# Two graph convolutions of a four-layer graph network: 90 of 125 superblocks placed and swept by cells, the rows of the other blocks fetched by GpSimd inside the same sweep

## The chip, the cores and the metric

The kernel runs on one core of a Trainium2 chip. A core has five engines that run side by side, each with its own instruction queue: TensorE (PE, the matrix multiplier), VectorE (DVE), ScalarE (ACT), GpSimd (POOL) and SyncE (SP, which only starts transfers); they wait for each other by semaphores. The metric is the time of one execution on the device, in microseconds, as the median of three runs.

## What is computed

A graph of 12,500 nodes with 32 features and 400,000 edges (`src`, `dst`) goes through four layers; each ends with a residual and a layer norm. The change touches the third, two graph convolutions in a row:

```python
def gcn_conv(x, W, b, row, col, n_nodes):
    xw = x @ W
    deg = jax.ops.segment_sum(ones, col, num_segments=n_nodes)
    dinv = jnp.where(deg > 0, jax.lax.rsqrt(deg), 0.0)
    norm = dinv[row] * dinv[col]
    msgs = norm[:, None] * xw[row]
    out = jax.ops.segment_sum(msgs, col, num_segments=n_nodes)
    return out + b
...
h = jax.nn.relu(gcn_conv(x, W1, b1, row, col, n))
h = jax.nn.relu(gcn_conv(h, W2, b2, row, col, n))
```

What costs time is `segment_sum(xw[row], col)`, once for each convolution: for each edge the row of its source is read and added to the row of its target. The norms are applied to whole nodes before and after.

## The kernel before

The edges are cut into 625 blocks of 640 (5 tiles of 128). The targets of a block lie close together, within a window of 64 nodes. Five blocks make a superblock, so there are 125.

The layers on either side (`weighted_edges`, `coupled_edges`) and `conv_edges` go block by block. POOL fetches the source rows with five indirect transfers (128 rows of 128 bytes each), DVE makes a one-hot matrix of the targets (`onehot`, 128x320), PE multiplies rows by one-hot, and DVE adds the resulting window to the sums.

The two convolutions share another way. `place_edges` runs once and sorts the edges of each superblock into cells: source node `100*row + bin` goes to bin `bin`, and each of the 100 bins has 64 places. Its loop over 125 superblocks (`rank_and_spread`, L1024 to L1058) is a chain of DVE instructions, with two POOL instructions (L896, L900) and 52 matmuls beside it. It stores, for each superblock, the source row of each place (`cells`) and the target (`cell_dst`). Edges that found no place stay in `rest`.

`cell_sweep` then runs once for each convolution, over the 125 superblocks, each in two halves of 50 bins. SP loads the source rows of a half, broadcast to all partitions (`src`, L1141, 800 KB). DVE compares them with the lane number (`from_row`, L1213) and makes 25 one-hot tiles of targets (`to_dst`, L1220, 128x224, bf16). PE picks the rows out of a table that stays in SBUF (`gather`, L1163, 50 matmuls a half), ACT copies them to SBUF (L1201), PE multiplies them by `to_dst` (`scatter`, L1176, 25 matmuls a half), and DVE adds the sum to `conv_acc` (L1231). The order is written out by hand: DVE makes half h+1 and then adds half h; PE runs two packs of gathers ahead of its scatters. POOL does nothing here. After each sweep `conv_edges` takes what is left in `rest`, here one turn of four blocks (L1287, L1307, L1321).

The address of each add comes from a table in SBUF that DVE's sequencer loads into registers (`base_of`, L406).

## Time and profile before

| | us |
|---|---|
| median of three runs | 18041.62 (18037.58 to 18050.91) |
| the profiled execution | 18071.57 |
| its span, first to last instruction | 18069.8 |
| stages up to the placing | 8258 |
| `place_edges` | 2129 |
| first sweep, with its preparation | 1572 |
| `conv_edges` and the node stage between | 231 |
| second sweep, with its preparation | 1577 |
| the rest | 4303 |

The profile gives each instruction's engine, start, duration and idle time before it. A name with `<-` reads "output from inputs", and L and a number is the line in the listing above. A pack of matmuls is shown as one row with a count. An f32 matmul is recorded twice (x10 are five matmuls).

### The profile page before, as it was taken

The numbers are of one execution on the slowest core, as the hardware profiler recorded it, in microseconds if no ns is written. First come the engines' busy times: TensorE is split into PE (matmuls) and PEld (weight loads), VectorE is DVE, ScalarE is ACT, GpSimd is POOL, SyncE is SP. The second block draws the span as 40 slices with busy tenths as digits, with TensorE's granted clock in tenths as the row PEclk, the third lists the DMA queues.
The fourth block names the chain that finished last, engine by engine and source line by source line (L and its number), as shares of the span: only waits on it lengthen the run. The fifth ranks groups of instructions, "written<-read, shape, count | busy, mean of one in ns | idle before, by whom it ended". The sixth has DMA issues, their size and how long they took to land. (4 is left out here: it accounts for less than half of the span.)

```text
span 18069.8 us, 315870 instructions
## 1 busy us (share of the span) xinstructions
PE 13832.7 (77%) x90210; PEld 10270.1 (57%) x90210; DVE 14107.8 (78%) x36234; ACT 3512.3 (19%) x6730; POOL 9545.5 (53%) x9706
## 2 busy tenths in 40 slices
PE   7999999997777777774333377777777999999998
PEld 5666666666666666664222255555555555555555
DVE  8999999983333333338999999959998999989996
ACT  1111111111000000001000044434443222222222
POOL 6777777774777777771222200000002777777774
PEclk9888888885555555555555599979998999999998
DMA  1111111110111111110000033313332111111111
GB/s 37 28 28 28 28 28 28 28 27 15 17 17 17 17 17 17 17 17 9 1 1 1 1 129 134 133 62 129 133 133 68 18 18 18 18 18 18 18 18 15
DMA packets 996527, 680.08 MB, mean 38 GB/s; under 512 B 743750, under 2 KB 911411, under 8 KB 995988
## 3 DMA queue, kind: packets, MB, share of 16 engines
q1 hardware_dynamic: 694254, 524.34, 9.9%
q0 software_dynamic: 302240, 155.35, 6.0%
q8 instruction: 15, 0.25, 0.0%
q14 instruction: 18, 0.15, 0.0%
HBM read 669.12 MB, written 9.60 MB: 38 GB/s over the span
## 5 line engine op out<-in xcount | busy, mean ns | idle before, releaser
L529 PE MATMUL weighted_weights_ps<-weighted_w_out,weighted_hidden 128*128 128x256 f32 x12600 | 3891.1, 436 | 591.0 <-DVE weighted_to_s L654 515.0
L529 PEld LDWEIGHTS weighted_weights_ps<-weighted_w_out,weighted_hidden 128*128 128x128 f32 x12600 | 2328.3, 205 | 2444.8 <-issue 1634.8
L740 PE MATMUL coupled_win<-coupled_onehot,coupled_prod 128*125 128x64 f32 x12500 | 2785.3, 419 | 1142.7 <-DVE coupled_prod L788 1142.7
L359 POOL DMA_INDIRECT weighted_rows<-x_after_convolved,weighted_idx x3140 | 3039.3, 968 | 1045.6 <-issue 942.9
L359 POOL DMA_INDIRECT weighted_rows<-in_x,weighted_idx x3140 | 3028.3, 964 | 1013.6 <-issue 935.5
L725 POOL DMA_INDIRECT coupled_rows<-x_after_weighted,coupled_idx x3125 | 2955.5, 946 | 1146.0 <-issue 952.3
L740 PEld LDWEIGHTS coupled_win<-coupled_onehot,coupled_prod 128*125 128x125 f32 x12500 | 2670.8, 329 | 1257.2 <-DVE coupled_prod L788 1257.2
L1220 DVE TENSOR_SCALAR cells_to_dst<-from,cells_current 128x224 bf16<-128x224 bf16 x12500 | 2389.9, 273 | 18.1
L784 DVE TENSOR_TENSOR coupled_prod<-coupled_harm,coupled_rows 128x640 f32<-128x640 f32 x625 | 515.4, 825 | 2381.1 <-DMA coupled_rows<-x_after_weighted,coupled_idx 2381.1
L1176 PE MATMUL cells_sum_ps<-cells_to_dst,cells_rows 128*96 128x224 bf16 x12500 | 1703.6, 267 | 687.6 <-DVE cells_to_dst L1220 687.6
L649 DVE TENSOR_TENSOR weighted_v_v<-weighted_weights_ps,weighted_scaled 128x320 f32<-128x320 f32 x3768 | 1956.2, 573 | 0.0
L1287 POOL DMA_INDIRECT conv_rows<-conv_rows,conv_idx x40 | 38.0, 950 | 3421.4 <-DMA conv_idx<-in_src_blocks 3409.8
L1201 ACT ACTIVATE cells_rows<-cells_rows_ps 128x480 bf16<-128x480 f32 x2500 | 1427.4, 571 | 1733.2 <-PE cells_rows_ps L1163 1733.2
L562 PEld LDWEIGHTS weighted_win_ps<-weighted_onehot,weighted_prod 128*128 128x128 f32 x12560 | 1712.3, 203 | 88.1
L1176 PEld LDWEIGHTS cells_sum_ps<-cells_to_dst,cells_rows 128*96 128x96 bf16 x12500 | 1132.2, 122 | 885.5 <-ACT cells_rows L1201 738.6
L562 PE MATMUL weighted_win_ps<-weighted_onehot,weighted_prod 128*128 128x64 f32 x12560 | 1624.4, 279 | 0.0
L519 PE MATMUL weighted_hid_ps<-weighted_feat,weighted_w_in 32*64 32x320 f32 (+1 forms) x3786 | 1531.4, 485 | 82.7 <-DMA weighted_feat<-in_ef 79.2
L578 ACT ACTIVATE weighted_hidden<-weighted_hid_ps,weighted_b_in 64x320 f32<-64x320 f32 x1262 | 659.4, 523 | 3338.4 <-PE weighted_hid_ps L519 3332.9
L1163 PE MATMUL cells_rows_ps<-cells_parts,cells_from_row 125*64 125x96 bf16 x25000 | 1010.2, 211 | 73.5 <-DVE cells_from_row L1213 73.5
L654 DVE TENSOR_TENSOR weighted_to_s<-weighted_weights_ps,weighted_scaled 128x640 f32<-128x640 f32 x1256 | 1020.4, 812 | 0.0
L661 DVE TENSOR_REDUCE weighted_prod<-weighted_to_s 128x40 f32<-128x640 f32 x1256 | 1016.1, 809 | 0.0
L578 ACT ACTIVATE weighted_hidden<-weighted_hid_ps,weighted_b_mid 64x320 f32<-64x320 f32 x1262 | 659.3, 522 | 1824.8 <-PE weighted_hid_ps L517 1824.8
(204 smaller groups left out, 14514.0 us busy)
## 6 DMA issues: line engine op xcount, KB each, us to landing
cells_src<-cell_sources SPq DMA_DIRECT2D x500, 800.0 KB, 4.1
weighted_feat<-in_ef SPq DMA_DIRECT2D x635, 80.0 KB
weighted_rows<-in_x,weighted_idx POOLq DMA_INDIRECT x3140
weighted_rows<-x_after_convolved,weighted_idx POOLq DMA_INDIRECT x3140
coupled_rows<-x_after_weighted,coupled_idx POOLq DMA_INDIRECT x3125, 2.4
weighted_idx<-in_src_blocks SPq DMA_DIRECT2D x1264, 2.5 KB
weighted_sh<-in_sh SPq DMA_DIRECT2D x1264, 10.0 KB
coupled_sh<-in_sh SPq DMA_DIRECT2D x630, 22.5 KB
```

The lines of the kernel that those rows point to most:

```text
L359: pool.indirect_dma_start(rows[s][:, t, :], None, table, bass.IndirectOffsetOnAxis(ap=idx[s][:, t:t + 1].bitcast(U32), axis=0))\
L519: mm = pe.matmul(hid_ps[0:halves * HID, 0:HALF], w_in[:, :], feat[slot][:, u * HALF:(u + 1) * HALF], start=True, stop=True)
L529: mm = pe.matmul(banks[bank][:, t * WPATHS:(t + 1) * WPATHS], hidden[slot][:, t * P:(t + 1) * P], w_out[:, :], start=True, stop=True)
L562: mm = pe.matmul(win_ps[0:MSG, 0:WINDOW], prod[s][:, t, :], onehot[s][:, t, :], start=(t == 0), stop=(t == TILES - 1))
L578: step = nc.scalar.activation(hidden[slot][0:HID, half * HALF:(half + 1) * HALF], hid_ps[0:HID, 0:HALF], func, bias=(b_mid if deep else b_ ...
L649: last = dve.tensor_tensor(v_v[:, :, m * MUL:(m + 1) * MUL, :], w_vv, v_m[:, :, None, :].broadcast_to([P, TILES, MUL, MUL]), ALU.mult)
L654: dve.tensor_tensor(to_s[:, :, :, :], w_s, scaled[:, :, None, 0:2 * MUL].broadcast_to([P, TILES, MUL, 2 * MUL]), ALU.mult).then_inc(w_used, 1)
L725: pool.indirect_dma_start(rows[s][:, t, :], None, table, bass.IndirectOffsetOnAxis(ap=idx[s][:, t:t + 1].bitcast(U32), axis=0))\
L740: mm = pe.matmul(win_ps[s][0:OCH, c * WINDOW:(c + 1) * WINDOW], prod[s][:, t, c * OCH:(c + 1) * OCH], onehot[s][:, t, :], start=(t == 0), ...
L1176: mm = pe.matmul(sum_ps[h][0:wide, 0:DSTS], rows[b][:, c, :], to_dst[h][:, t, :], start=(t == 0), stop=(t == HALF_TILES - 1))
L1201: nc.scalar.activation(rows[b][:, :, :].rearrange("p c f -> p (c f)"), rows_ps[b][:, 0:PACK * wide], ACT.Copy).then_inc(copied, 1)
L1220: made = dve.tensor_scalar(to_dst[h][:, t, :], k["from1"][:, 0:DSTS], current[h][:, t:t + 1], None, ALU.is_equal)
```

## The change

The placing and both sweeps cover only the first 90 superblocks (450 blocks). The other 178 blocks (175 real ones and 3 that are empty) go by rows, two beside each of the superblocks 0 to 88 of each sweep. For each of them SP loads the source numbers, POOL fetches the rows with five indirect transfers into one of four slots, DVE makes a 128x320 one-hot, PE does five f32 matmuls into a PSUM bank of its own (`win_ps`), and DVE adds the 32x64 window to the first 32 partitions of `conv_acc`. The three addresses of a superblock's adds are loaded together. In `place_edges` two instructions over 875 columns mark which edges of these blocks fall outside the window.

```diff
+COVERED = 90
+BY_CELL = COVERED * SUPER
+BY_ROW = BLOCKS - BY_CELL
+ROW_SLOTS = 4
...
-            k["super_lo"] = held("super_lo", [1, SUPERS], I32)
+            k["add_at"] = held("add_at", [1, COVERED, 3], I32)
...
-            cell_sweep(nc, a, k, "cells1", cells)
+            cell_sweep(nc, a, k, "cells1", cells, u1)
...
+                then(dve.tensor_copy(k["add_at"][:, :, 0:1], lo_super[0:1, :, None]))
+                then(dve.tensor_copy(k["add_at"][:, 0:BY_ROW // 2, 1:3],
+                                     k["lo"][:, BY_CELL:].rearrange("o (n b) -> o n b", b=2)))
...
-                with dve.Fori(0, SUPERS // 2, 1) as i:
+                with dve.Fori(0, COVERED // 2 - 1, 1) as i:
...
+                by_row = src_f[:, ALL:].rearrange("p (b t) -> p b t", t=TILES)
+                dve.tensor_scalar(by_row, k["local"][:, BY_CELL:REAL_BLOCKS, :], float(WINDOW), -1e6, ALU.is_lt,
+                                  ALU.mult).then_inc(step, 1)
+                dve.wait_ge(step, done + 1)
+                dve.tensor_tensor(k["rest"][:, BY_CELL:REAL_BLOCKS, :], k["local"][:, BY_CELL:REAL_BLOCKS, :], by_row,
+                                  ALU.add).then_inc(step, 1)
...
+        idx = [sb(f"idx{s}", [P, TILES], I32) for s in range(ROW_SLOTS)]
+        onehot = pair(sb, "onehot", [P, TILES, WINDOW])
+        fetched = [sb(f"fetched{s}", [P, TILES, FEAT]) for s in range(ROW_SLOTS)]
+        win_ps = psum("win", [P, 512])
+        idx_loaded, started, hot = [sem(f"idx_loaded{s}") for s in range(ROW_SLOTS)], sem("started"), sem("hot")
+        landed = [sem(f"landed{s}") for s in range(ROW_SLOTS)]
+        win_spread, win_added = sem("win_spread"), sem("win_added")
+        PAIRS = (COVERED - 1) // 2
...
+                def number(i, q):
+                    sp.dma_start(idx[q][:, :], one(a["src_blocks"], i * ROW_SLOTS + (BY_CELL + q))).then_inc(idx_loaded[q], 16)
+
+                def super_of(i, s, more):
+                    n = i * 2 + s
                     for h in range(2):
                         sp.wait_ge(row_ready, n * 2 + h + 1)
                         fill(n + 1, h)
+                    if more:
+                        for b in range(2):
+                            sp.wait_ge(win_spread, n * 2 + (b + 1 + ROW_SLOTS))
+                            number(i + 1, s * 2 + b)
+
+                for h in range(2):
+                    fill(0, h)
+                for q in range(ROW_SLOTS):
+                    number(0, q)
+                with sp.Fori(0, PAIRS - 1, 1) as i:
+                    for s in range(2):
+                        super_of(i, s, True)
...
+            @block.gpsimd
+            def _(pool):
+                def fetch(i, s):
+                    hold(pool, win_spread, i * ROW_SLOTS + s + 1, started)
+                    hold(pool, idx_loaded[s], i * 16 + 16, started)
+                    for t in range(TILES):
+                        pool.indirect_dma_start(fetched[s][:, t, :], None, table,
+                                                bass.IndirectOffsetOnAxis(ap=idx[s][:, t:t + 1].bitcast(U32), axis=0))\
+                            .then_inc(landed[s], 16)
+
+                with pool.Fori(0, PAIRS, 1) as i:
+                    for s in range(ROW_SLOTS):
+                        fetch(i, s)
+                for s in range(2):
+                    fetch(PAIRS, s)
...
+                def spread_rows(i, q):
+                    j = i * ROW_SLOTS + q
+                    pe.wait_ge(win_added, j + 1)
+                    pe.wait_ge(hot, j + 1)
+                    pe.wait_ge(landed[q], i * (16 * TILES) + 16 * TILES)
+                    for t in range(TILES):
+                        mm = pe.matmul(win_ps[0:FEAT, 0:WINDOW], fetched[q][:, t, :], onehot[q % 2][:, t, :],
+                                       start=(t == 0), stop=(t == TILES - 1))
+                    mm.then_inc(win_spread, 1)
+                def super_of(i, s):
+                    n = i * 2 + s
                     for g in range(PACKS):
                         gather(n + (g + AHEAD) // PACKS, (g + AHEAD) % PACKS)
                         scatter(n, g)
+                        if g % HALF_PACKS == 2:
+                            spread_rows(i, s * 2 + g // HALF_PACKS)
...
+                def one_hot(n, b):
+                    rows = k["local"][:, bass.ds(n * 2 + (BY_CELL + b), 1), :].rearrange("p b t -> p (b t)")
+                    wide_hot = [P, TILES, WINDOW]
+                    dve.tensor_tensor(onehot[b][:, :, :], k["iota0"][:, None, :].broadcast_to(wide_hot),
+                                      rows[:, :, None].broadcast_to(wide_hot), ALU.is_equal).then_inc(hot, 1)
+                def add_rows(n, b, at):
+                    dve.wait_ge(win_spread, n * 2 + (b + 1 + ROW_SLOTS))
+                    dve.wait_ge(summed, n * 2 + (b + 3))
+                    dst = k["acc"][0:FEAT, 0, bass.ds(at, WINDOW)]
+                    dve.tensor_tensor(dst, dst, win_ps[0:FEAT, 0:WINDOW], ALU.add).then_inc(win_added, 1)
+                def super_of(n):
+                    one_hot(n, 0)
+                    half(n, 1)
+                    at = nc_values(nc, k["add_at"][0:1, bass.ds(n, 1), :].rearrange("o n c -> o (n c)"))
+                    dve.wait_ge(win_added, n * 2 + 1)
+                    add(n, 0, at[0])
+                    add_rows(n, 0, at[1])
+                    one_hot(n, 1)
+                    half(n + 1, 0)
+                    dve.wait_ge(win_added, n * 2 + 2)
+                    add(n, 1, at[0])
+                    add_rows(n, 1, at[2])
+                dve.sem_inc(win_added, 1)
                 half(0, 0)
-                with dve.Fori(0, SUPERS - 1, 1) as n:
-                    half(n, 1)
-                    at = base_of(n)
-                    add(n, 0, at)
-                    half(n + 1, 0)
-                    add(n, 1, at)
-                half(SUPERS - 1, 1)
-                at = base_of(SUPERS - 1)
-                add(SUPERS - 1, 0, at)
-                add(SUPERS - 1, 1, at)
+                with dve.Fori(0, COVERED - 1, 1) as n:
+                    super_of(n)
...
```

On DVE, in the loop of the sweep, these rows stand from the second half's `from_row` to the add of the first half (ISA and REGISTER_ALU are address and counter work of the sequencer, TENSOR_LOAD loads addresses), before:

```order
L1213 TENSOR_SCALAR cells_from_row<-cells_src,lane 128x3200
L1215 ISA
L1215 COPY cells_current<-cell_dst 128x25
L1218 ISA
L1220 TENSOR_SCALAR cells_to_dst<-from,cells_current 128x224 x25
L406 ISA
L406 TENSOR_LOAD super_lo
L406 ISA x2
L1228 REGISTER_ALU
L1231 ISA
L1231 TENSOR_TENSOR conv_acc<-conv_acc,cells_sum_ps 96x224
```

and after, from the load to the next block's one-hot:

```order
L410 TENSOR_LOAD add_at
L410 ISA x6
L1320 REGISTER_ALU
L1298 REGISTER_ALU
L1301 ISA
L1301 TENSOR_TENSOR conv_acc<-conv_acc,cells_sum_ps 96x224
L1311 REGISTER_ALU
L1312 REGISTER_ALU
L1314 ISA
L1314 TENSOR_TENSOR conv_acc<-conv_acc,cells_win_ps 32x64
L1307 ISA
L1307 TENSOR_TENSOR cells_onehot<-iota,local 128x320
```

A window's add and a one-hot now stand behind each half's add, and one load takes three addresses. On PE, in the same loop, the third pack of a half before:

```order
L1163 MATMUL cells_rows_ps<-cells_parts,cells_from_row 64x96 x10
L1173 REGISTER_ALU
L1176 MATMUL cells_sum_ps<-cells_to_dst,cells_rows 96x224 x5
L1158 REGISTER_ALU
L1163 MATMUL cells_rows_ps<-cells_parts,cells_from_row 64x96 x10
```

and after:

```order
L1216 MATMUL cells_rows_ps<-cells_parts,cells_from_row 64x96 x10
L1226 REGISTER_ALU
L1229 MATMUL cells_sum_ps<-cells_to_dst,cells_rows 96x224 x5
L1236 ISA
L1238 ISA
L1240 MATMUL cells_win_ps<-cells_onehot,cells_fetched 32x64 x5
L1211 REGISTER_ALU
L1216 MATMUL cells_rows_ps<-cells_parts,cells_from_row 64x96 x10
```

The five matmuls on fetched rows, with their waits, stand between the third and the fourth pack of each half.

## Rows read from the trace of the kernel before

**Rows 1.** Busy time by engine in two stretches: the placing, the first sweep.
```profile
core 0: us, PE busy (x) PEld busy (x) DVE busy (x) ACT busy (x) POOL busy (x), PEclk, DMA share, GB/s
8258.00:10387.00 2129.00, 668.72 (x6500) 609.23 (x6500) 2078.87 (x1650) 48.45 (x250) 481.86 (x250) 0.53 0.01 1
10387.00:11959.00 1572.00, 1197.19 (x18750) 901.32 (x18750) 1554.87 (x7006) 713.70 (x1250) 0.00 (x0) 0.99 0.36 130
```
**Rows 2.** Line L1057: duration min/median/max, first and last start.
```profile
L1057 DVE TENSOR_TENSOR place_at<-place_at_rank,place_dst x125: 1809/1811/1818, 8301.4 to 10367.5; 128x1600 bf16<-128x1600 bf16 x125
```
**Rows 3.** Timeline of one half (start, duration, engine, line, pack, idle before).
```profile
11202.60 0.38 DVE L1231 TENSOR_TENSOR conv_acc<-conv_acc,cells_sum_ps 96x224 f32 x1
...
11202.82 0.68 PE L1176 MATMUL cells_sum_ps<-cells_to_dst,cells_rows 128*96 128x224 bf16 x5 [1.37 <-DVE cells_to_dst L1220]
11202.90 1.04 DVE L1213 TENSOR_SCALAR cells_from_row<-cells_src,lane 128x3200 bf16<-128x3200 bf16 x1
...
11203.75 0.68 PE L1176 MATMUL cells_sum_ps<-cells_to_dst,cells_rows 128*96 128x224 bf16 x5
...
11204.07 4.78 DVE L1220 TENSOR_SCALAR cells_to_dst<-from,cells_current 128x224 bf16<-128x224 bf16 x25
...
11208.76 0.38 DVE L1231 TENSOR_TENSOR conv_acc<-conv_acc,cells_sum_ps 96x224 f32 x1
```
**Rows 4.** Timeline: the first sweep's first `from_row` and its last add.
```profile
10413.91 1.05 DVE L1213 TENSOR_SCALAR cells_from_row<-cells_src,lane 128x3200 bf16<-128x3200 bf16 x1
...
11958.03 0.39 DVE L1231 TENSOR_TENSOR conv_acc<-conv_acc,cells_sum_ps 96x224 f32 x1 [3.32 <-PE cells_sum_ps L1176]
```
**Rows 5.** Timeline in `conv_edges`, where blocks go by rows.
```profile
11965.14 0.89 DVE L399 TENSOR_TENSOR conv_onehot<-conv_iota,rest 128x320 f32<-128x320 f32 x2 [3.98 <-issue]
...
11970.36 1.27 PE L1307 MATMUL conv_win<-conv_onehot,conv_rows 128*32 128x64 f32 x10 [12.37 <-DMA conv_rows<-conv_rows,conv_idx]
11970.51 0.94 POOL L1287 DMA_INDIRECT conv_rows<-conv_rows,conv_idx  x1 [0.30 <-issue]
...
11971.85 0.21 DVE L1321 TENSOR_TENSOR conv_acc<-conv_acc,conv_win 32x64 f32 x1 [5.82 <-PE conv_win L1307]
11972.00 0.49 DVE L399 TENSOR_TENSOR conv_onehot<-conv_iota,rest 128x320 f32<-128x320 f32 x1
```
**Rows 6.** Line L406, address loads on DVE's sequencer: ns min/median/max.
```profile
L406 DVEq TENSOR_LOAD <-super_lo x250: 300/304/325, 10423.7 to 13760.4; - x125
...
L406 DVEq TENSOR_LOAD <-conv_base x2: 978/981/984, 11962.9 to 13771.6; - x2
```
**Rows 7.** Timelines where DVE and GpSimd meet: gathers with a cast, then the placing.
```profile
69.48 0.95 POOL L359 DMA_INDIRECT weighted_rows<-in_x,weighted_idx  x1 [0.30 <-issue]
70.03 0.70 DVE L380 CAST weighted_base<-weighted_base_f 1x629 int32<-1x629 f32 x1
...
4261.14 1.00 POOL L725 DMA_INDIRECT coupled_rows<-x_after_weighted,coupled_idx  x1 [0.30 <-issue]
4261.35 0.48 DVE L380 CAST coupled_base<-coupled_base_f 1x629 int32<-1x629 f32 x1
...
9300.11 1.81 DVE L1050 TENSOR_TENSOR place_at_rank<-from,place_rank 128x1600 bf16<-128x1600 bf16 x1
9300.42 2.65 POOL L896 TENSOR_TENSOR place_others<-place_later,place_bin_of 128x625 bf16<-128x625 bf16 x1 [0.26 <-POOL place_gap L900]
9301.84 1.27 DVE L1053 TENSOR_TENSOR rest<-local,place_cov 128x25 f32 x1
```
**Rows 8.** Transfers: size, and median us from issue to landing.
```profile
cells_src<-cell_sources SPq DMA_DIRECT2D x500, 800.0 KB, 4.1
...
conv_idx<-in_src_blocks SPq DMA_DIRECT2D x16, 2.5 KB, 1.6
```
**Rows 9.** Timeline of PE's first packs of the first sweep.
```profile
10421.70 1.17 PE L1176 MATMUL cells_sum_ps<-cells_to_dst,cells_rows 128*96 128x224 bf16 x5
...
10423.34 0.93 PE L1176 MATMUL cells_sum_ps<-cells_to_dst,cells_rows 128*96 128x224 bf16 x5
```

More of the change, by code:

```diff
@@ L945, in _ @@
                         turn(i * 2 + s, s)
-                count(SUPERS - 1, 0)
-                place(SUPERS - 2, 1)
-                turn(SUPERS - 3, 0)
-                place(SUPERS - 1, 0)
-                turn(SUPERS - 2, 1)
-                turn(SUPERS - 1, 0)
+                place(COVERED - 1, 1)
+                turn(COVERED - 2, 0)
+                turn(COVERED - 1, 1)
             @block.scalar
@@ L976, in _ @@
                     copy_dst(i * 2 + 1)
-                copy_dst(SUPERS - 1)
+                copy(COVERED - 1, 1, COVERED // 2 - 1)
+                copy_dst(COVERED - 2)
+                copy_dst(COVERED - 1)
             @block.vector
@@ L1178, in scatter @@
                     mm.then_inc(spread, 1)
-                pe.sem_inc(gathered, PACKS)
-                pe.sem_inc(spread, PACKS)
-                for g in range(AHEAD):
-                    gather(0, g)
-                with pe.Fori(0, SUPERS - 1, 1) as n:
+                def spread_rows(i, q):
[9 more added lines that the diff above has]
+                    n = i * 2 + s
                     for g in range(PACKS):
```

88 lines of the change are left out of this document (50 added, 38 removed).

## The prediction

> **What bounds the kernel now.** I read the busy time by stretches first, since the change touches only three of them, and then the timelines inside. In the placing DVE is busy 2079 of 2129 us, in the first sweep 1555 of 1572 us, where POOL does nothing [rows 1]; the second sweep repeats it. Both stages are DVE's, and each is a loop with a fixed period, so I count in periods. The placing starts the same instruction 125 times between 8301.4 and 10367.5 [rows 2]: 2066.1 / 124 = 16.66 us per superblock. In a sweep the reader should see DVE without a hole: add at 11202.60, `from_row` at 11202.90, 25 `to_dst`, next add at 11208.76 [rows 3]. Half a superblock is 6.16 us, a whole one 12.32. PE does its five packs of a half 0.93 to 0.94 us apart, 4.7 us, and then sits idle 1.37 us until DVE has made the next `to_dst` [rows 3]. A sweep takes from 10413.91 to 11958.42 [rows 4], 1544.5 us.
>
> **What the change removes.** 35 of 125 superblocks go. Placing: 35 x 16.66 = 583 us. Its preparation and its last step work on whole tables of 3125 columns, of which the first become 2250 and two instructions over 875 columns are new; I take 4 us of gain, with 0 and 8 as bounds. Each sweep: 35 x 12.32 = 431 us, two sweeps 862. Without any addition that is 583 + 4 + 862 = 1449 us.
>
> **What it adds on DVE, the engine that sets the period.** Beside each of the superblocks 0 to 88 there are now two blocks by rows. (1) Two one-hots 128x320: two in a row take 0.89 us and the second lasts 0.49 [rows 5], so each costs 0.40 to 0.41 between neighbours, 0.8 for two. (2) Two adds 32x64: the next instruction starts 0.15 us after one [rows 5], 0.3 for two; before each stands a wait for the add just issued, which empties the pipe; I give 0.1 each, bounds 0 to 0.2 (an add of 0.38 overlaps its follower by 0.08 in rows 3). (3) One load of three addresses where one address was loaded. One took 0.30 us on the sequencer, four took 0.98 [rows 6], and the register work behind it goes from 2 rows to 6. Today all this is hidden behind `to_dst` already queued, as DVE runs without a hole. I take 0.2 exposed, bounds 0 and 0.7. Sum of the fixed part: 0.8 + 0.3 + 0.2 + 0.2 = 1.5 us per superblock, bounds 1.1 and 2.2.
>
> **What GpSimd's gathers do to DVE.** This is the term that no row shows directly: nowhere in the trace of before do gathers run beside a stream of bf16 `tensor_scalar`. The nearest rows are single casts. A cast that takes 0.48 us took 0.70 when it began 0.55 us into a gather, and the gather kept its 0.95; another cast that began 0.21 us into a gather kept its 0.48, and that gather took 1.00 [rows 7]. So the two exclude each other for a part of the gather. The later cast ended 0.30 us after the gather, the same cast unhindered needs 0.48; counting back, it got through about 0.85 into the gather. The other gather was held back by 0.05 by a cast that ended at 0.69. I estimate an exclusive stretch of 0.25 us in each gather, from about 0.6 to 0.85. Ten gathers in a superblock would block 2.5 us; DVE is in `from_row` and `to_dst` 5.86 of a half that will last some 7.8 us, three quarters of the time, which makes 1.9 us. One-hots and adds are not hindered as far as the trace shows. I take 1.8, since a `to_dst` leaves short gaps of its own; bounds 0.5 (the gaps swallow most of it) and 3.5 (each gather also breaks the overlap of two neighbours).
>
> Here the Trainium skill speaks against the change. The page "SBUF — State Buffer", section "Who interferes with whom", says that VectorE in a two-port mode and GpSimd, writing descriptors for its own transfers, take a shared pair of ports in turns, and the one that comes second waits out the other's whole instruction. Rows 7 agree on the direction, but show 0.22 and 0.05 us, not a whole gather. The same page (section "A bandwidth-pool intuition that's wrong") has a transfer of 620 ns becoming one of 3100 ns beside a long copy; by that ratio, as an estimate, a gather would take 4.7 us, a superblock 50 and the kernel some 23,400. That is rival C below at its far end; the rest of this text does without it.
>
> **What it adds elsewhere.** PE gets ten f32 matmuls a superblock; a block took 1.27 us at most [rows 5]. A half then holds 4.7 + 1.27 = 6.0 us of PE work; DVE's half becomes 7.8, so PE stays hidden, with 1.8 us idle. Even in today's half the idle 1.37 would hold the 1.27. POOL: a gather of 0.94 with 0.30 between [rows 5] is 1.25 us, ten are 12.5 us, with four waits on its queue some 13, against a period of 15.6: hidden, with 2.6 us to spare. SP loads the source numbers, 2.5 KB in 1.6 us, behind loads of 800 KB that land in 4.1 [rows 8]. On its queue the wait for a block's matmuls now stands ahead of the next superblock's loads; these matmuls come at the third pack of a half, at most 4 us after `from_row`, and the data are wanted a period later, so nothing waits. A slot's round (numbers 1.6 to 6, five gathers 6.3, landing about 2.5) is at most 15 us and has two periods, 31.
>
> **Sum.** The new period is 12.32 + 1.5 + 1.8 = 15.6 us. A sweep becomes 1544.5 - 431 + 89 x 3.3 = 1407 us, a gain of 137; two give 275. With the placing 275 + 583 + 4 = 862 us. The profiled execution took 18071.6, so 17210 would be its successor; it lies 30 us over the median of the runs, against which I forecast **17180 us**.
>
> **Rivals.**
>
> (A) The gathers cost DVE next to nothing (0.5), and the rest comes out at its low bound 1.1: 1.6 us per superblock, sweep 1256, total 16877. For it: the first cast of rows 7 lost nothing and the gather 0.05. Against it: the second lost 0.22.
>
> (B) POOL sets the pace. If each gather has to wait for a gap in `to_dst` and comes every 1.75 us instead of 1.25, ten and the waits take 17.8 us, the period is 17.8, a sweep 1113 + 89 x 5.5 = 1603, and the kernel takes 18042 - 587 + 2 x 58 = 17571. For it: only 2.6 us of slack per superblock on POOL. Against it: the gather in rows 7 that lost most lost 0.05.
>
> (C) **Slower: DVE starves POOL.** In `to_dst` 25 instructions overlap without a gap. If GpSimd gets its turn only when DVE does something else (one gather in the 1 us of adds and one-hot), eight of ten gathers are left, and DVE then waits for them at `add_rows`: 2 x (6.16 + 0.75) + 8 x 1.25 = 23.8 us per superblock, a sweep 1113 + 89 x 11.5 = 2136, total 18042 - 587 + 2 x 592 = 18639. The kernel is slower than before once the period passes 12.32 + 1449 / 178 = 20.5 us. For it: in the placing a GpSimd instruction beside DVE lasted 2.65 us. Against it: that very place. The DVE instruction at 9300.11 ended at 9301.92, and the next, issued at 9301.84 and only 25 columns wide, lasted 1.27, until GpSimd's was done [rows 7]. GpSimd gets in between neighbours.
>
> (D) TensorE's clock. In the sweep the granted clock is 0.99, which is 2.4 GHz, and in the placing, with PE busy a third of the time, 0.53, near 1.2 GHz [rows 1]. PE's idle time per half grows from 1.4 to 1.8 us. At the lower clock, in the sweep's first packs, they come 1.64 us apart [rows 9]: 16.4 + 2.5 = 18.9 us per superblock, PE sets the period, sweep 1113 + 89 x 6.6 = 1700, total 17766. Against it: at that pace PE is never idle, which is how the clock rose at the start.
>
> (E) The change doesn't do what it says: blocks by rows leave edges over, and `conv_edges` runs 157 turns instead of one: 20 gathers of 1.25 us are 25 us a turn, 3900 us for each convolution, and the kernel takes some 25,000. Against it: every block goes through the row-wise stages before and after in one pass over its window of 64 already.
>
> **How the numbers follow.** Forecast case 0.58; its own bounds, with the gathers' term at 0.8 to 3 and the rest at 1.2 to 2, are 2.0 to 5.0 us a superblock, 16950 to 17480; A 0.13; B 0.13; C 0.09; D 0.05; E 0.02. The range takes in A, B and the near edge of D: 16850 to 17700, and leaves out C, E and parts of the ends. A measurement of this kernel tells 0.2%, 36 us, from no change. Faster is everything but C and E: 0.88. Within 0.2%: 0.01. Slower: 0.11.
>
> **What would show each step.** The placing's period must stay 16.66 over 90 turns; `to_dst` beside gathers should show a mean above 0.273, or gaps of 0.1 to 0.3 us, ten times a superblock; the distance of two same adds should be 15.6 (13.9 is A, 17.8 B, 23.8 C). Gathers should keep 0.95 to 1.1 us; over 1.4 speaks for B or C. DVE's waits in the sweep for the matmuls on fetched rows should be near zero. The granted clock in the sweep should stay at 0.99. Most likely to be wrong is the 1.8 us: every microsecond per superblock is 178 us in the result.

## The result, and the profile after

The changed kernel takes 17002.54 us, the median of four runs (16993.83 to 17020.48); the kernel before, beside it on the same chip, takes 18044.54 (18037.58 to 18050.91). The ratio is 0.9424, 95% interval 0.9408 to 0.944. The forecast was 17180 in a range of 16850 to 17700, so the direction and the range held, and the gain was 1042 us instead of 862. The profiled execution took 16993.83 us, against 18071.57 before.

The two stretches of [rows 1], now of the kernel after (the placing, then the first sweep):

```profile
core 0: us, PE busy (x) PEld busy (x) DVE busy (x) ACT busy (x) POOL busy (x), PEclk, DMA share, GB/s
8237.00:9785.00 1548.00, 481.52 (x4680) 438.68 (x4680) 1499.94 (x1199) 34.93 (x180) 347.85 (x184) 0.53 0.01 2
9785.00:11128.00 1343.00, 1072.15 (x15280) 819.29 (x15280) 1271.73 (x5402) 513.81 (x900) 950.78 (x890) 0.91 0.39 121
```

The line that answers to [rows 2] gives the placing's period:

```profile
L1061 DVE TENSOR_TENSOR place_at<-place_at_rank,place_dst x90: 1808/1811/1818, 8284.0 to 9764.6; 128x1600 bf16<-128x1600 bf16 x90
```

1480.6 / 89 = 16.64 us, as before; from the first of these rows to the last it is 1480.6 us instead of 2066.1, 585.5 less. The first sweep's first `from_row` and last add [rows 4] are now:

```profile
9811.60 1.06 DVE L1286 TENSOR_SCALAR cells_from_row<-cells_src,lane 128x3200 bf16<-128x3200 bf16 x1 [0.22 <-DVE conv_acc L1279]
...
11126.97 0.38 DVE L1301 TENSOR_TENSOR conv_acc<-conv_acc,cells_sum_ps 96x224 f32 x1 [4.79 <-PE cells_sum_ps L1229]
```

That is 1315.8 us instead of 1544.5, 228.7 less; the second sweep, read in the same way, lost 225. Together with the placing 1039 us, which is the whole gain of the medians. Removing 35 superblocks took 431 from a sweep, so the rows beside the other 89 give back 431 - 227 = 204 us: 2.3 us a superblock in the mean of both sweeps, where the forecast had 3.3.

One superblock on DVE, where [rows 3] showed half of one (start, duration, line, idle before):

```profile
10999.57 1.05 DVE L1286 TENSOR_SCALAR cells_from_row<-cells_src,lane 128x3200 bf16<-128x3200 bf16 x1
11000.53 0.17 DVE L1288 CAST cells_current<-cell_dst 128x25 f32 x1
11000.74 4.90 DVE L1293 TENSOR_SCALAR cells_to_dst<-from,cells_current 128x224 bf16<-128x224 bf16 x25
11005.57 0.38 DVE L1301 TENSOR_TENSOR conv_acc<-conv_acc,cells_sum_ps 96x224 f32 x1
11006.09 0.21 DVE L1314 TENSOR_TENSOR conv_acc<-conv_acc,cells_win_ps 32x64 f32 x1
11006.24 0.49 DVE L1307 TENSOR_TENSOR cells_onehot<-iota,local 128x320 f32<-128x320 f32 x1
11006.65 1.05 DVE L1286 TENSOR_SCALAR cells_from_row<-cells_src,lane 128x3200 bf16<-128x3200 bf16 x1
...
11012.65 0.37 DVE L1301 TENSOR_TENSOR conv_acc<-conv_acc,cells_sum_ps 96x224 f32 x1
11013.16 0.21 DVE L1314 TENSOR_TENSOR conv_acc<-conv_acc,cells_win_ps 32x64 f32 x1
11013.68 0.49 DVE L1307 TENSOR_TENSOR cells_onehot<-iota,local 128x320 f32<-128x320 f32 x1 [0.32 <-issue]
11014.09 1.05 DVE L1286 TENSOR_SCALAR cells_from_row<-cells_src,lane 128x3200 bf16<-128x3200 bf16 x1
```

The period is 14.52 us (10999.57 to 11014.09) against 12.32. That is a superblock of the first sweep; in the second the loop's top shows 0.35 us of "issue" where this one has 0.32, and over a whole sweep the mean from one `from_row` of a superblock to the next one's is 14.57 us in the first and 14.64 in the second. The 2.20 us between them can be read off start by start. The one-hot delays its follower by 0.41, twice 0.82. The window add delays its follower by 0.15, twice 0.30. From an add to the window add behind it there are 0.52 us, where the next instruction used to start after 0.30: 0.22 of waiting for the result just issued, twice 0.44. At the loop's top 0.37 more (0.52 instead of 0.15 behind the window add, 0.31 to 0.32 of it shown as "issue"). And the run of 25 `to_dst` goes from 4.69 to 4.83 from its start to the next add, twice 0.28. The sum is 2.21.

On POOL the gathers of the same sweep (an excerpt of its timeline):

```profile
10502.37 0.94 POOL L1195 DMA_INDIRECT cells_fetched<-conv_rows,cells_idx  x1 [0.30 <-issue]
10503.61 1.37 POOL L1195 DMA_INDIRECT cells_fetched<-conv_rows,cells_idx  x1 [0.30 <-issue]
...
10509.81 1.60 POOL L1195 DMA_INDIRECT cells_fetched<-conv_rows,cells_idx  x1 [0.90 <-DMA cells_idx<-in_src_blocks]
```

and on the page all of them, with `to_dst`:

```profile
L1195 POOL DMA_INDIRECT cells_fetched<-conv_rows,cells_idx x1780 | 1900.4, 1068 | 983.6 <-DMA cells_idx<-in_src_blocks 473.1
L1293 DVE TENSOR_SCALAR cells_to_dst<-from,cells_current 128x224 bf16<-128x224 bf16 x9000 | 1759.2, 292 | 13.1
```

A gather lasts 1068 ns in the mean, against 0.94 in [rows 5]. A single `to_dst` is recorded with 292 ns instead of 273, but the starts of two neighbours are hardly further apart, as the run of 25 shows.

### The profile page after: what moved, and what is told of

The parts are those of the page before. It is cut to its first block and busy times, and to the rows that moved or that the text cites. A ratio compares the mean times of both kernels' runs of the same rounds, so it can differ in the third digit from the quotient of the medians.

```text
span 16991.9 us, 294438 instructions
## 1 busy us (share of the span) xinstructions
PE 13403.3 (79%) x81450; PEld 9938.5 (58%) x81450; DVE 12959.6 (76%) x32574; ACT 3098.8 (18%) x5960; POOL 11277.9 (66%) x11416
## 5 line engine op out<-in xcount | busy, mean ns | idle before, releaser
L744 PE MATMUL coupled_win<-coupled_onehot,coupled_prod 128*125 128x64 f32 x12500 | 2785.3, 419 | 1135.4 <-DVE coupled_prod L792 1135.4
L744 PEld LDWEIGHTS coupled_win<-coupled_onehot,coupled_prod 128*125 128x125 f32 x12500 | 2670.8, 329 | 1249.9 <-DVE coupled_prod L792 1249.9
L1195 POOL DMA_INDIRECT cells_fetched<-conv_rows,cells_idx x1780 | 1900.4, 1068 | 983.6 <-DMA cells_idx<-in_src_blocks 473.1
L1293 DVE TENSOR_SCALAR cells_to_dst<-from,cells_current 128x224 bf16<-128x224 bf16 x9000 | 1759.2, 292 | 13.1
L1229 PE MATMUL cells_sum_ps<-cells_to_dst,cells_rows 128*96 128x224 bf16 x9000 | 1324.3, 282 | 493.9 <-DVE cells_to_dst L1293 492.2
L1274 ACT ACTIVATE cells_rows<-cells_rows_ps 128x480 bf16<-128x480 f32 x1800 | 1027.6, 571 | 1679.5 <-PE cells_rows_ps L1216 1569.1
L1229 PEld LDWEIGHTS cells_sum_ps<-cells_to_dst,cells_rows 128*96 128x96 bf16 x9000 | 883.7, 130 | 644.9 <-issue 437.8
L521 PE MATMUL weighted_hid_ps<-weighted_first,weighted_w_mid 128*64 128x320 f32 x2524 | 962.7, 463 | 2.8 <-ACT weighted_first L579 2.1
```

What stands on the lines that cost most here:

```text
L744: mm = pe.matmul(win_ps[s][0:OCH, c * WINDOW:(c + 1) * WINDOW], prod[s][:, t, c * OCH:(c + 1) * OCH], onehot[s][:, t, :], start=(t == 0), ...
L1195: pool.indirect_dma_start(fetched[s][:, t, :], None, table, bass.IndirectOffsetOnAxis(ap=idx[s][:, t:t + 1].bitcast(U32), axis=0))\
L1229: mm = pe.matmul(sum_ps[h][0:wide, 0:DSTS], rows[b][:, c, :], to_dst[h][:, t, :], start=(t == 0), stop=(t == HALF_TILES - 1))
L1274: nc.scalar.activation(rows[b][:, :, :].rearrange("p c f -> p (c f)"), rows_ps[b][:, 0:PACK * wide], ACT.Copy).then_inc(copied, 1)
L1293: made = dve.tensor_scalar(to_dst[h][:, t, :], k["from1"][:, 0:DSTS], current[h][:, t:t + 1], None, ALU.is_equal)
```

## The experiments

They ran in three groups, each group on a chip of its own with the kernel before beside it. On the chip of the second group the kernel before took 18116.76 us (median of nine), nearly what it took for the result. The first and the third group met two other chips, on which it took 22188.41 and 22259.58 us (13 runs each). I call these two chips of the second kind and the other one of the first kind; what the second kind does differently has its own part below. So that kernels of both kinds of chip can be laid side by side, I read one number from each trace: the distance from one clearing of `conv_acc`, at the start of the first sweep, to the next, at the start of the second. For the kernel after it is this row:

```profile
L1279 DVE MEMSET conv_acc<- x2: 10662/10662/10662, 9800.7 to 11379.8; 96x12724 f32 x2
```

so 1579.1 us. It holds the whole first sweep, with 11 us ahead of it and 252 to 254 us behind it in every trace of the table. All kernels read so:

| kernel | distance, us | ratio to before, 95% interval |
|---|---|---|
| before | 1807.1 | 1 |
| after | 1579.1 | 0.9424 (0.9408 to 0.944) |
| after_again | 1574.9 | 0.9423 (0.9407 to 0.944) |
| cells_only_2 | 1376.8 | 0.9191 (0.9176 to 0.9206) |
| onehot_first | 1517.9 | 0.9337 (0.9321 to 0.9352) |
| six_gathers | 1739.6 | 0.9587 (0.9568 to 0.9606) |
| cells_only (second kind) | 1378.1 | 0.9335 (0.93 to 0.937) |
| rows_by_sync, rows_by_sync_2 (second kind) | 1551.3, 1552.1 | 0.9503 (0.9478 to 0.9527), 0.9485 (0.9469 to 0.9501) |
| onehot_sync (second kind) | 1499.4 | 0.947 (0.9449 to 0.9491) |
| matmuls_twice, matmuls_twice_2 (second kind) | 2088.7, 2101.1 | 1.0 (0.9986 to 1.0015), 1.0007 (0.9995 to 1.002) |
| before_gathers, before_gathers_2 (second kind) | 3459.7, 3463.3 | 1.148 (1.1451 to 1.1509), 1.1505 (1.1486 to 1.1524) |

Where DVE sets the pace and POOL does not gather, the two kinds agree to 1.3 us (1376.8 and 1378.1). The theory to be tested: beside the cells, rows cost DVE its own instructions and waits (1.9 us a superblock) and next to nothing for the port that it shares with GpSimd. Its rivals: the prediction's split (1.5 fixed, 1.8 for the gathers) with something else that came out smaller; POOL as a pace setter; TensorE not quite hidden.

### The rows' whole price: cells_only

All work on the rows is left out, in POOL, SP, PE and DVE; the output lacks those edges' part.

```diff
-                    one_hot(n, 0)
                     half(n, 1)
                     add(n, 0, at[0])
-                    add_rows(n, 0, at[1])
-                    one_hot(n, 1)
                     half(n + 1, 0)
                     add(n, 1, at[0])
-                    add_rows(n, 1, at[2])
```

> The changed kernel, in which the sweeps' blocks by rows are left out on all engines (no numbers loaded, no gathers, no matmuls on fetched rows, no one-hots, no window adds); the edges of 178 blocks are missing from the output. Theory 1 (all that the rows cost is on DVE in the loop): the period falls from 14.52 us back to 12.32, a sweep from 1316 to 90 x 12.32 + 4 = 1113 us, and the kernel from 17003 to about 16595. Theory 2 (something else of the change, such as the table of addresses, also costs): the period stays above 12.4 and the kernel above 16620.

> The changed kernel without the work of the rows: POOL gathers nothing, no one-hots, no row matmuls, no window adds, in both sweeps; only the cells of 90 superblocks are summed. If the rows cost what the changed kernel's trace shows over the old period (14.5 against 12.32 us), this runs its 89 periods at 12.32 us and is 2 x 90 x 2.2 = 400 us faster than the changed kernel. If part of that was the smaller sweep's own loop, the period stays above 12.32 us and the gain is below 350 us.

On a chip of the second kind 20737.31 us (20669.75 to 20802.83), on one of the first 16657.18 (16631.93 to 16665.75), where the kernel after once more took 17059.02 (16986.47 to 17091.65): 402 us for the rows. The expectation's 16595 went with 17003 for the kernel after and was 408 below it. The timeline of cells_only_2:

```profile
10504.61 1.04 DVE L1262 TENSOR_SCALAR cells_from_row<-cells_src,lane 128x3200 bf16<-128x3200 bf16 x1
...
10510.47 0.38 DVE L1277 TENSOR_TENSOR conv_acc<-conv_acc,cells_sum_ps 96x224 f32 x1
10510.76 1.04 DVE L1262 TENSOR_SCALAR cells_from_row<-cells_src,lane 128x3200 bf16<-128x3200 bf16 x1
```

A half is 6.15 us again, as in [rows 3]. So the cells cost what they did, and the 2.2 us are the rows' alone.

> The changed kernel once more, unedited, as the measure for the three kernels beside it. Where the kernel before takes 18,044 us, it should take 17,003 us (ratio 0.942) as measured; on a chip that takes over 22,000 us for the kernel before, the same 1,040 us less would be a ratio of 0.953.

It came as expected, ratio 0.9423.

### Without the gathers: rows_by_sync

POOL's five gathers of a block become one transfer of as many rows by SP, the table's first rows, so other data and another output.

```diff
-                    sp.dma_start(idx[q][:, :], one(a["src_blocks"], ...)).then_inc(idx_loaded[q], 16)
+                    sp.dma_start(fetched[q][:, :, :], table[0:BLOCK, :].rearrange("(t p) f -> p t f", p=P)).then_inc(landed[q], 16)
```

> The changed kernel, in which SyncE fills each slot with one plain transfer of 640 consecutive rows, and GpSimd does nothing in the sweeps; the rows fetched are not those of the edges. DVE and PE do all that they do in the changed kernel. Theory 1 (GpSimd's gathers cost DVE 0.3 us a superblock): period 14.2 instead of 14.5, kernel 16945 to 16960. Theory 2 (the prediction's 1.8 us were right and the rest cheaper than thought): period 12.7 to 13.0, kernel about 16700. The gap of 0.15 to 0.5 us between the add and the window's add stays by theory 1.

> The changed kernel with POOL's five gathers of a block replaced by one transfer of as many rows from SP (the table's first rows, so other data); POOL does nothing in the sweeps, all else stands. From the changed kernel's trace the gathers cost the vector engine 0.14 us in a run of 25 one-hots and 0.04 us in a gather one-hot, so 0.3 to 0.4 us of 14.5 a superblock: about 16,950 us where the changed kernel takes 17,003 to 17,059, 55 to 75 us less. By the prediction's port term (1.8 us a superblock) it would be 320 us less. If twelve gathers set the pace and ten already do now and then, some 20 us more go.

Each ran on one of the chips of the second kind: 21102.51 us (21059.9 to 21123.58) and 21116.07 (21099.79 to 21170.99). Since the kernel after did not run there, I compare sweeps and not totals, across the two kinds of chip. The timeline of rows_by_sync_2, one half with the loop's top ahead of it:

```profile
13006.32 0.49 DVE L1291 TENSOR_TENSOR cells_onehot<-iota,local 128x320 f32<-128x320 f32 x1 [0.31 <-issue]
13006.73 1.05 DVE L1270 TENSOR_SCALAR cells_from_row<-cells_src,lane 128x3200 bf16<-128x3200 bf16 x1
...
13012.59 0.37 DVE L1285 TENSOR_TENSOR conv_acc<-conv_acc,cells_sum_ps 96x224 f32 x1
13013.11 0.21 DVE L1298 TENSOR_TENSOR conv_acc<-conv_acc,cells_win_ps 32x64 f32 x1
13013.27 0.49 DVE L1291 TENSOR_TENSOR cells_onehot<-iota,local 128x320 f32<-128x320 f32 x1
13013.68 1.05 DVE L1270 TENSOR_SCALAR cells_from_row<-cells_src,lane 128x3200 bf16<-128x3200 bf16 x1
```

This half is 6.95 us instead of 7.08, and the other one, with the loop's top (12999.42 to 13006.73), 7.31 instead of 7.44. The period is 14.26 instead of 14.52: ten gathers cost DVE 0.26 us, 0.026 each, as the expectation's 14.2 had it and far from the 12.7 to 13.0 of the prediction's split. The sweep agrees: 1574.9 to 1579.1 against 1552.1 is 23 to 27 us for 89 superblocks, 0.26 to 0.30. The 0.22 between the two adds and the 0.31 at the loop's top stand unchanged where POOL does nothing, so they are not the gathers'.

### The waits between neighbours: onehot_first

```diff
                 def super_of(n, more=True):
-                    one_hot(n, 0)
                     half(n, 1)
                     add(n, 0, at[0])
-                    add_rows(n, 0, at[1])
                     one_hot(n, 1)
+                    add_rows(n, 0, at[1])
                     half(n + 1, 0)
                     add(n, 1, at[0])
+                    if more:
+                        one_hot(n + 1, 0)
                     add_rows(n, 1, at[2])
```

> The first one-hot of a superblock is written ahead of the window add, between the add of the sums and the add of the rows, and that of the next superblock at the end of this one, so that no vector instruction stands right behind the one whose result it needs. Theory 1, the 0.67 us between the add's start and the window add's start (0.30 us before, with no window add) is the wait of the second on the first: 0.37 us twice a superblock go, perhaps also the 0.3 us at the loop's top, so 0.7 to 1.1 us for each of 179 superblocks, 130 to 190 us less than the changed kernel. Rival, the gap is the making of the address and the loop's own turn: no change within 20 us.

16907.11 us (16855.62 to 16923.71), 152 below the kernel after on the same chip, and the fastest kernel of this study that computes everything. The timeline:

```profile
10211.18 1.05 DVE L1286 TENSOR_SCALAR cells_from_row<-cells_src,lane 128x3200 bf16<-128x3200 bf16 x1 [0.19 <-issue]
...
10217.16 0.38 DVE L1301 TENSOR_TENSOR conv_acc<-conv_acc,cells_sum_ps 96x224 f32 x1
10217.46 0.48 DVE L1307 TENSOR_TENSOR cells_onehot<-iota,local 128x320 f32<-128x320 f32 x1
10217.86 0.20 DVE L1314 TENSOR_TENSOR conv_acc<-conv_acc,cells_win_ps 32x64 f32 x1
10217.99 1.03 DVE L1286 TENSOR_SCALAR cells_from_row<-cells_src,lane 128x3200 bf16<-128x3200 bf16 x1
...
10225.08 1.05 DVE L1286 TENSOR_SCALAR cells_from_row<-cells_src,lane 128x3200 bf16<-128x3200 bf16 x1 [0.19 <-issue]
```

Behind the add the one-hot starts after 0.30 us, and the window add behind the one-hot without a wait. The period is 13.90, 0.62 less. The 0.22 of each half is gone, which is 0.44, and the "issue" at the loop's top falls from 0.31 to 0.19, another 0.12; something at the loop's top remains. In the second sweep the top gains more: from 0.35 us to a hole of 0.08 (11711.88 to 12.16, with a window add of 0.20), at a period of 13.78. What the 0.22 is, is not parted by this edit: the code makes the window add wait for the add's result, but a third instruction also hides the sequencer's own work ahead of the window add (two REGISTER_ALU and an ISA). For the wait speaks that the distance of 0.52 is the same where the add stood queued behind `to_dst` and where it had itself started late (after: 11028.23, 0.98 behind, then 11028.75). My expectation of 0.7 to 1.1 took the whole 0.37 from the add to the one-hot as the wait, in which the window add's own 0.15 was counted too. From the first `from_row` of the first sweep to the last of the second the kernel is 132.8 us shorter (2752.3 against 2885.1), 0.75 for each of 178 superblocks, more than 0.62 because of the second sweep; the rest of the 152 is within the spread of the runs.

### POOL's margin: six_gathers

Each block gets a sixth gather, into a spare tile.

```diff
-                    for t in range(TILES):
-                        pool.indirect_dma_start(fetched[s][:, t, :], None, table, ...
+                    for t in range(TILES + 1):
+                        into, t = (fetched[s][:, t, :], t) if t < TILES else (spare[s][:, :], 0)
+                        pool.indirect_dma_start(into, None, table, ...
```

> Each block of rows is fetched with six gathers instead of five, the sixth into a spare tile that nothing reads; everything else stands. By the trace of the changed kernel a superblock takes 14.5 us, 10 gathers with their gaps some 11 to 12. If POOL is hidden to the end, twelve gathers (12 times 1.07 to 1.37 = 12.8 to 16.4 us) straddle the period: no change at the low end, and at the high end POOL sets the pace at 16.4 us, 1.9 us more for each of 178 superblocks, 340 us. If instead each gather costs the vector engine its share of the port term (0.3 us by ten), the two more cost 0.06 us a superblock, 10 us in all. The prediction's own 0.18 us a gather would be 64 us.

17370.08 us (17339.73 to 17394.33), 311 more than the kernel after beside it. POOL's and DVE's rows of the first sweep say where it went:

```profile
L1197 POOL DMA_INDIRECT cells_fetched<-conv_rows,cells_idx x867 | 904.0, 1043 | 264.3 <-issue 264.0 <-DMA cells_idx<-in_src_blocks 0.3
L1197 POOL DMA_INDIRECT cells_spare<-conv_rows,cells_idx x173 | 200.1, 1157 | 52.7 <-issue 52.7
...
L1303 DVE TENSOR_TENSOR conv_acc<-conv_acc,cells_sum_ps 96x224 f32 x175 | 66.0, 377 | 152.1 <-PE cells_sum_ps L1231 152.1
```

A gather and the gap behind it take (904.0 + 264.3 + 200.1 + 52.7) / 1040 = 1.37 us, and twelve 16.4. The sweep grew by 160.5 to 164.7 us, 1.8 a superblock, which makes the period 14.5 + 1.8 to 1.9 = 16.4. POOL never waits for anything here but the gaps between its own gathers; DVE waits for PE's sums, and PE's row matmuls wait for the landing of the sixth gather (221.4 us in 99 waits of the first sweep): twelve gathers set the pace. Ten at the same 1.37 take 13.7 of the 14.5 us, so in the kernel after POOL should be hidden by 0.8 us, not by the 2.6 of the prediction. Its own trace agrees: in the first sweep the 890 gathers and their gaps take (950.8 + 239.0 + 19.5) / 890 = 1.36 us each, and POOL waits 79.5 us for numbers in the 88 superblocks from 9840, 0.9 each. DVE's part in the 311 us is the other rival's 10 us at most.

### Both edits: onehot_sync

> The two edits together: the one-hots between the two adds, and the rows by SP's transfers in place of POOL's gathers (other data). The half of the vector engine is 6.75 to 6.8 us in the trace of the first edit alone, where POOL's ten gathers take 13.2 to 13.5 us and its idle time is only their gaps. If POOL's gathers now set the pace beside the vector engine, taking them away gives 0.1 to 0.3 us beyond the port term: a period of 13.3, and 16,830 us or less, 75 us or more below the first edit alone. If the vector engine alone sets it, only the port term goes, 0.2 to 0.3 us a superblock, 40 to 55 us.

It leaves out the gathers as rows_by_sync does and has the order of onehot_first. On a chip of the second kind 21071.3 us (21033.06 to 21123.17), ratio 0.947 (0.9449 to 0.9491), where rows_by_sync_2 has 0.9485: the intervals of the totals overlap, the sweeps do not. The distance between the clearings is 1499.4 us, 52.7 below rows_by_sync_2 (0.59 a superblock: the edit of onehot_first, gathers or not) and 18.5 below onehot_first (0.21 a superblock: the gathers, again). The timeline has a period of 13.65 (13004.85 to 13018.50, in halves of 6.94 and 6.71) against 13.90. That is the port term alone, the size that rows_by_sync found. So POOL did not hold the vector engine back in onehot_first; DVE waited there 8.7 us for PE's sums in both sweeps together, as in cells_only_2 (9.0). But POOL had nothing left to give, as its row of onehot_first from 10000 to 11000 shows:

```profile
L1195 POOL DMA_INDIRECT cells_fetched<-conv_rows,cells_idx x720 | 781.4, 1085 | 219.4 <-issue 204.8 <-PE cells_win_ps L1240 14.3 <-DMA cells_idx<-in_src_blocks 0.3
```

That is 720 gathers in 1000 us, 13.9 for ten, as long as the period, and the idle time is one gap of 0.30 behind each, whatever it is put down to.

### Whether TensorE has room: matmuls_twice

Each block's row matmuls are made twice, the same output.

```diff
-                    for t in range(TILES):
-                        mm = pe.matmul(win_ps[0:FEAT, 0:WINDOW], fetched[q][:, t, :], onehot[q % 2][:, t, :], ...)
+                    for _ in range(2):
+                        for t in range(TILES):
+                            mm = pe.matmul(win_ps[0:FEAT, 0:WINDOW], fetched[q][:, t, :], onehot[q % 2][:, t, :], ...)
```

> The changed kernel, with the five f32 matmuls on fetched rows done twice (the second time with the same result). Adds 0.75 us of PE a half at 2.4 GHz. Theory 1 (PE's work on rows lies in its idle time of 1.4 to 2 us a half): period 14.5, kernel within 20 us of 17003. Theory 2 (the cover is thin, because the granted clock has fallen to 0.91): DVE waits for PE in many halves, and the kernel gains 50 to 150 us.

> The changed kernel with each block's five row matmuls made twice in a row, so the same output. If TensorE's row work (0.74 us a block in the trace) is hidden in a half of 7.3 us, in which TensorE waits 1.6 to 2.0 us for the vector engine, doubling it costs nothing: within 30 us of the changed kernel, and the idle time before the sums' matmuls falls by 0.7 us a half. If TensorE is the bound at its lower granted clock, it costs 2 x 0.74 us for each of 178 superblocks, up to 260 us.

22199.13 us (22147.76 to 22241.67) and 22253.14 (22204.64 to 22315.64), one on each chip of the second kind. Neither theory covers it: the sweep is 510 to 526 us longer than that of the kernel after, 5.8 a superblock, where doubling should cost 1.5 at most. The first sweep of matmuls_twice_2, and two stretches of PE's timeline in it:

```profile
12500.00:14100.00 1600.00, 1242.48 (x14855) 923.46 (x14855) 1092.11 (x4684) 428.01 (x783) 822.80 (x781) 0.83 0.28 88
```

```profile
13708.36 1.30 PE L1241 MATMUL cells_win_ps<-cells_onehot,cells_fetched 128*32 128x64 f32 x20
13709.59 0.40 PE L1216 MATMUL cells_rows_ps<-cells_parts,cells_from_row 125*64 125x96 bf16 x10
...
13718.91 0.29 PE L1216 MATMUL cells_rows_ps<-cells_parts,cells_from_row 125*64 125x96 bf16 x4 [0.32 <-issue]
13719.66 0.25 PE L1216 MATMUL cells_rows_ps<-cells_parts,cells_from_row 125*64 125x96 bf16 x2 [0.47 <-issue]
13720.43 0.21 PE L1216 MATMUL cells_rows_ps<-cells_parts,cells_from_row 125*64 125x96 bf16 x1 [0.52 <-issue]
```

A pack of ten that takes 0.40 us falls apart into fours, twos and ones, 0.75 us from start to start, and no semaphore explains the holes. So this run says nothing on the room that PE has on a chip of the first kind. What the trace of after shows there, over the first sweep: a block's row matmuls take 0.74 us, PE waited 166 times for `to_dst` before the sums' matmuls, 1.4 us in the mean (233.2 in all) and 2.1 at most, and DVE waited for the sums 7.4 us in all. Doubling them there was not run.

### Gathers beside the old sweep: before_gathers

The kernel before, with ten gathers a superblock that nothing reads; the output is right.

```diff
+            @block.gpsimd
+            def _(pool):
+                with pool.Fori(0, SUPERS - 3, 1) as n:
+                    for s in range(2):
+                        hold(pool, landed[s], n * (16 * TILES) + 16 * TILES, started)
+                        fetch(s)
```

> The kernel before, with ten gathers a superblock added on GpSimd in both sweeps (1240 each sweep), into buffers that nobody reads. Nothing else is added. This measures alone what gathers cost a DVE that streams to_dst. Theory 1 (0.3 to 0.4 us a superblock, as the changed kernel's lengths suggest): period 12.65, kernel about 18125. Theory 2 (the prediction: an exclusive 0.25 us in each gather, hit three times in four or more): period 14.2 to 14.8, kernel 18500 to 18650. Rival C of the prediction (GpSimd starved): gathers of several us each, DVE's period unchanged at 12.3 while GpSimd runs on after the sweep.

> The kernel before with ten gathers a superblock in both sweeps that nothing reads or waits for: the vector engine's work is the old one. By the changed kernel's trace (0.3 us for ten gathers) 250 superblocks lose 75 us, ratio 1.004. By the prediction's term (1.8 us for ten) they would lose 450 us, 1.025. POOL needs 13.5 us for ten (twelve need 16.2), more than the period of 12.32, so each sweep is followed by a tail of 125 x 1.2 = 150 us in which the gathers end: 300 us more by either theory, if nothing covers it, so 1.02 against 1.04. What decides is the half's length in the trace, 6.16 us without gathers.

25495.81 us (25490.13 to 25525.85) and 25601.22 (25574.41 to 25616.44), against 22188.41 and 22259.58: both far off either theory, and both on chips of the second kind. In two stretches of the first sweep of before_gathers_2, with the gathers and after their end:

```profile
core 0: us, PE busy (x) PEld busy (x) DVE busy (x) ACT busy (x) POOL busy (x), PEclk, DMA share, GB/s
13450.00:13650.00 200.00, 19.63 (x71) 9.27 (x71) 6.55 (x28) 2.85 (x5) 154.12 (x143) 0.50 0.09 16
...
14850.00:15050.00 200.00, 154.97 (x2434) 116.60 (x2430) 198.88 (x913) 92.93 (x163) 0.00 (x0) 1.00 0.37 134
```

and PE inside the first:

```profile
13501.56 0.24 PE L1186 MATMUL cells_rows_ps<-cells_parts,cells_from_row 125*64 125x96 bf16 x1 [2.56 <-issue]
13505.07 0.24 PE L1186 MATMUL cells_rows_ps<-cells_parts,cells_from_row 125*64 125x96 bf16 x1 [3.27 <-issue]
13507.86 0.24 PE L1186 MATMUL cells_rows_ps<-cells_parts,cells_from_row 125*64 125x96 bf16 x1 [2.55 <-issue]
```

The reader is to see the counts: 71 matmul records in 200 us beside 143 gathers, 2434 without any. PE does one matmul each 2 to 3.5 us while POOL gathers without a pause, at a DMA share of 0.09. DVE is idle because PE is. The price of the port, for which the kernel was made, is buried under this; rows_by_sync measures it. On a chip of the first kind this kernel was not run.

## Why the prediction held, and which step was off

**What goes.** Right: the placing's period 16.64 (forecast 16.66), 585.5 us less from its first row to its last (forecast 583, and 587 with its preparation); the cells' own period still 12.3 without rows (cells_only_2).

**The fixed part.** 1.93 us instead of 1.5, inside its bounds of 1.1 to 2.2. The one-hots (0.82 for 0.8) and the adds (0.30 for 0.3) were right. The wait for the add just issued was mis-sized: 0.22 each, where 0.1 was given with 0.2 as the bound, and onehot_first recovers it. The loop's top cost 0.37 for 0.2, in the bounds. Whether that is the load of three addresses, their register work or the extra waits is not settled; the runs show that it stands without gathers, and that another order alone shrinks the "issue" there from 0.31 to 0.19 in the first sweep and from 0.35 to 0.08 in the second.

**The port.** This step failed, the exclusive stretch of 0.25 us in each gather, charged to DVE: 1.8 us a superblock was given, with 0.5 as the low bound, and it is 0.26 (rows_by_sync_2) to 0.28 (the timeline of after), outside the bounds. The step took the stretch out of two casts, each a single long instruction, and charged three quarters of it to DVE. In the sweep a `to_dst` starts every 0.19 us (4.83 / 25), and by the rows the one that bears most of the conflict is the gather: 1068 ns in the mean for the 0.94 us of [rows 5], and 1.37 and 1.60 in the two rows above that meet `from_row`, DVE's long instruction (the longest in this kernel is 1.77). The direction in which the argument of rival C pointed, GpSimd waiting for DVE, is the right one; its size is a tenth of a microsecond a gather. The sentence of the Trainium skill (page "SBUF — State Buffer", section "Who interferes with whom") that the second comer waits out the other's whole instruction fits GpSimd's side in part: `from_row`, with 1.05 us, stands beside the gathers of 1.37 and 1.60. It does not fit DVE's side: a `to_dst` starts every 0.19 us while gathers of 1 us are running, and 25 of them take 4.83 us instead of 4.69. The ratio of 620 to 3100 ns in that page's section "A bandwidth-pool intuition that's wrong" has nothing like it here (1.13 in the mean, 1.9 at most in the kernel after).

**The sum.** The period came to 14.52, between rival A's 13.9 and the forecast's 15.6. 0.43 too little in the fixed part and 1.5 too much in the port leave the forecast 1.1 us a superblock too high, 190 us over two sweeps; the result lay 178 below it. That the time fell into the range is owed to the 1449 us that went for certain and to the range's width, and in part to luck, as the two errors pulled against each other. It does not bear out the port term, which lies below even rival A's 0.5.

**The rest.** POOL was hidden, as said, but with 0.8 to 0.9 us to spare and not 2.6: of that 1.1 went with the shorter period, and the rest because 0.94 + 0.30 was read from gathers that met nobody, where they took 1.36 with their gap in the sweep. Rival B was two gathers away, as six_gathers shows, and in onehot_first POOL already runs without a pause. C and E did not come. D's premise half came: the granted clock in the sweep is 0.91, not the 0.99 that I said would stay, and it is 0.89 in six_gathers, 0.95 in onehot_first and 1.00 in cells_only_2; it cost nothing that can be read, as PE still waits for `to_dst` and DVE hardly for PE.

## What to carry to other kernels

Price a neighbour on a shared port for each instruction of the other side, not by the stretch of time: here a stream of short instructions went on nearly undisturbed, and the neighbour paid; then add that price to the neighbour's own period, since it may be what brings it to the edge. Two instructions on one engine where the second needs the first's result stood 0.2 us further apart than others, and an independent third one moved between them hid it; look for one to move there. And count the slack of the hidden engine from its rows in the busy stage, not from a quiet one.

## What the runs showed of the hardware that was not expected

The kernel before took 18044 to 18117 us where the result and the second group ran, and 22188 and 22260 us on the two chips of the second kind. The difference is not in the sweeps or the placing: the distance of the clearings in cells_only is 1378.1 us on the second kind and 1376.8 on the first, and the placing takes 1480.4 and 1480.6 from its first turn to its last. It is in the stages where POOL gathers beside a loop of many matmuls: line L744 runs from 5662.8 to 10767.5 on the second kind, 5105 us, and from 4272.5 to 8160.3 on the first, 3888. That line of the same kernel, in cells_only (second kind) and in cells_only_2 (first kind):

```profile
L744 PE MATMUL coupled_win<-coupled_onehot,coupled_prod 128*125 128x64 f32 x12500 | 2745.6, 401 | 2399.7 <-issue 2390.7
```

```profile
L744 PE MATMUL coupled_win<-coupled_onehot,coupled_prod 128*125 128x64 f32 x12500 | 2785.4, 419 | 1143.4 <-DVE coupled_prod L792 1143.4
```

PE is as busy, but its 1143.4 us of waiting for DVE became 2390.7 us of waiting for nothing that the profile shows. With before_gathers and matmuls_twice this looks like one pattern: on those chips PE starts its instructions late while POOL gathers, one in 2 to 3.5 us beside gathers that never pause, and at the usual rate as soon as they end. SP's plain transfers of as many rows do not do it (rows_by_sync_2 takes 1552.1 us). Gathers that never pause do not do it by themselves either: on a chip of the first kind those of onehot_first and six_gathers never do, and DVE sets the pace in the one and the gathers in the other. But before_gathers and matmuls_twice ran on the second kind alone, so that the chip is to blame for them too is not shown; only the pair of L744 shows it. That PE is supplied with instructions late, and that this supply and the gathers' transfers meet somewhere, is a guess; no row shows it. So what the change is worth on such a chip stays open: the kernel after itself was not run there, and a kernel that gives the sweeps gathers they did not have may gain less than 0.058 of its time.
